# A graph convolution on one core: the search for runs moves from VectorE to ScalarE, and the sorted edges are searched in blocks of 8 instead of 16

## The reference, cut to what matters

```python
msg = node_feat[src] + edge_feat                       # 400000 x 64
agg = segment_sum(msg, dst, num_segments=12500)        # 12500 x 64
h = relu(agg @ W1 + b1)                                # 12500 x 128
x = layernorm(x + (h @ W2 + b2))
```

## Time and the profile before

| what | value |
|---|---|
| median of 3 runs | 1467.95 us (1467.6 to 1469.04) |
| profiled execution | 1467.16 us, its span 1465.4 us |
| TensorE matmul busy | 1223.0 us, 83% |
| VectorE busy | 1217.6 us, 83% |
| GpSimd busy | 967.6 us, 66% |
| ScalarE busy | 751.7 us, 51% |
| mean granted TensorE clock | 0.906 of full |

### The profile page before, as it was taken

How to read it: one execution, slowest core, us unless ns; L and a number is a source line. 1 busy time by engine, 2 the same in 40 slices (tenths; PEclk the granted TensorE clock), 3 DMA queues, 4 the chain that set the end, 5 groups by cost and what they waited for, 6 DMA issues and landing times.

```text
span 1465.4 us, 47112 instructions
## 1 busy us (share of the span) xinstructions
PE 1223.0 (83%) x18748; PEld 1107.5 (76%) x18749; DVE 1217.6 (83%) x2696; ACT 751.7 (51%) x941; POOL 967.6 (66%) x1043
## 2 busy tenths in 40 slices
PE   1457878888888899888989899999999999999873
PEld 1356777776778888887878889888888888898642
DVE  5499888898988898989998888888889899887333
ACT  3734322233445455554455666666666666665252
POOL 6767777777676677777767667676666766674132
PEclk8566698899998999999999999999999999999975
DMA  6724444444443444444443434444333444332132
GB/s 166 177 77 126 114 128 117 113 128 121 110 120 104 117 114 120 112 123 109 105 127 105 119 102 107 117 108 110 108 104 103 123 113 111 101 100 64 33 76 67
DMA packets 157980, 161.09 MB, mean 110 GB/s; under 512 B 52803, under 2 KB 141955, under 8 KB 157427
## 3 DMA queue, kind: packets, MB, share of 16 engines
q1 hardware_dynamic: 126149, 123.61, 28.6%
q0 software_dynamic: 31616, 34.50, 12.4%
HBM read 153.06 MB, written 4.93 MB: 108 GB/s over the span
## 4 chain that ended last, share of the span: by engine, by line
PE 44%; DVE 28%; issue 17%; DVEq 5%; ACT 3%; DMA 2%; POOL 1%; POOLq 0%; SPq 0%
PE sums_ps L1175 20%; PE counted_ps L1158 12%; DVE oh_key L953 11%; PE chunk_ps L1140 10%; DVE oh_lo L949 8%; DVEq L907 3%; ACT counts L741 3%; DVE lists L918 2%; DVE onehot L893 2%; DMA lists<-in_dst 1%; DVEq L918 1%; POOL x_parts L658 1%; DVE less_b L843 1%; DMA edge_records<-counts 1%; PE turn_ps L1186 1%
## 5 line engine op out<-in xcount | busy, mean ns | idle before, releaser
L617 POOL DMA_INDIRECT xmsg<-in_x,idx_t x925 | 888.4, 960 | 292.4 <-issue 275.0
L741 ACT CAST counts<-counted_ps 128x784 bf16<-128x784 f32 (+2 forms) x728 | 618.3, 865 | 500.8 <-PE counted_ps L1158 494.3
L1158 PE MATMUL counted_ps<-oh_key,oh_lo 128*128 128x98 bf16 (+1 forms) x5264 | 579.4, 232 | 143.6 <-DVE oh_key L953 109.5
L1175 PE MATMUL sums_ps<-x_parts,counts 128*128 128x193 bf16 (+3 forms) x4900 | 629.0, 254 | 0.3
L1158 PEld LDWEIGHTS counted_ps<-oh_key,oh_lo 128*128 128x128 bf16 x5264 | 381.8, 103 | 204.8 <-DVE oh_key L953 149.9
L949 DVE TENSOR_TENSOR oh_lo<-chunk_ps,tables 128x768 bf16<-128x768 f16 (+3 forms) x622 | 444.6, 715 | 94.6 <-PE counted_ps L1158 57.8
L953 DVE TENSOR_TENSOR oh_key<-chunk_ps,tables 128x1176 bf16<-128x1176 f16 (+2 forms) x622 | 459.5, 739 | 0.0
L1175 PEld LDWEIGHTS sums_ps<-x_parts,counts 128*128 128x128 bf16 (+3 forms) x4900 | 455.8, 118 | 4.6 <-issue 3.1
L1140 PE MATMUL chunk_ps<-onehot,cmsg 128*64 128x16 f32 (+4 forms) x4400 | 167.3, 222 | 6.3 <-DVE lists L918 5.3
L1140 PEld LDWEIGHTS chunk_ps<-onehot,cmsg 128*64 128x64 f32 x4400 | 153.6, 147 | 22.6 <-issue 9.5
L918 DVE TENSOR_TENSOR lists<-lists,chunk_ps 64x48 f32 (+6 forms) x625 | 113.8, 182 | 30.5 <-PE chunk_ps L1140 8.4
(11 more groups left out here) (104 smaller groups left out, 459.6 us busy)
## 6 DMA issues: line engine op xcount, KB each, us to landing
cmsg<-in_edge_attr SPq DMA_DIRECT2D x440, 160.0 KB
gmsg<-in_edge_attr SPq DMA_DIRECT2D x185, 160.0 KB
xmsg<-in_x,idx_t POOLq DMA_INDIRECT x925
x_parts<-in_x SPq DMA_DIRECT2D x12, 256.0 KB, 3.2
out_nodes<-x_parts SPq DMA_DIRECT2D x12, 256.0 KB, 2.6
edge_records<-counts SPq DMA_DIRECT2D x1, 1500.0 KB
lists<-in_src SPq DMA_DIRECT2D x1, 1400.0 KB
lists<-in_dst SPq DMA_DIRECT2D x1, 1400.0 KB
```

The costliest lines, as they stand in the source:

```text
L617: pool.indirect_dma_start(xmsg[:, at * D:(at + 1) * D], None, x, bass.IndirectOffsetOnAxis(ap=idx_t[:, of:of + 1], axis=0)).then_inc(gathe ...
L741: nc.scalar.copy(to.rearrange("p h (m n) -> p h m n", m=m), ps.rearrange("p m (n h) -> p h m n", h=HI)).then_inc(unit_kept, 1)
L1158: mm = nc.tensor.matmul(unit_ps[u][:, col:col + slot.key_cols], oh_lo[s % RING][:, n * P:(n + 1) * P], oh_key[s % RING][:, n * slot.key_co ...
L1175: mm = nc.tensor.matmul(sums_ps[0:n, 0:XC], counts[b % 2][:, h * P:h * P + n], x_parts[:, h * XC:(h + 1) * XC], start=(h == 0), stop=(h == ...
```

## The change

1. FINE goes from 16 to 8. A record row is half as long and there are twice as many; the array of largest destinations is twice as long (SPAN). A run of 128 edges is 16 rows instead of 8, and the same bytes. `plan` may put up to 121 edges into a window instead of 113, and makes another plan.
2. The count of the search moves from VectorE to ScalarE. ScalarE computes Sign(node - 0.5 - most) over the array and accumulates it: (blocks below) - (blocks not below). The values are written over the array in place, as bf16, so `less_b` is gone. As the sum is twice the count minus the length, the row number is used in half records (`record_halves`).
3. VectorE keeps the small instruction that makes the row number, now `locate`, at T-6. ScalarE's `search` stands at T-8, the load at T-15, and `load_records` at T-4.
4. For the first two groups ScalarE searches between its copies of `idx` and of `rel`, and VectorE locates after it has computed `rel`.
5. The five loads of weights and biases go from the start of SyncE's program to its end, after the last search, as `w1_sb`, `w2_sb` and `b2_all` now share memory with `most_b`.

```diff
-FINE = 16
+FINE = 8
...
-    SEARCH_LOAD = at_slots([(max(0, TABLE_AT[g] - 13), g) for g in later])
-    SEARCH = at_slots([(max(0, TABLE_AT[g] - 6), g) for g in later])
+    SEARCH_LOAD = at_slots([(max(0, TABLE_AT[g] - 15), g) for g in later])
+    SEARCH = at_slots([(max(0, TABLE_AT[g] - 8), g) for g in later])
+    LOCATE = at_slots([(max(0, TABLE_AT[g] - 6), g) for g in later])
...
+    record_halves = record_dram.rearrange("r (h k) -> (r h) k", h=2)
...
-        less_b = sb("less_b", [P, SPAN], bf16)
+        node_half = sb("node_half", [P, GROUPS])
...
+            sp.wait_ge(searched, GROUPS)
+            for half in range(2):
+                sp.dma_start(w1_sb[half * D:(half + 1) * D, :], w1).then_inc(weights_in, 16)
+            sp.dma_start(w2_sb[:, :], w2).then_inc(weights_in, 16)
+            sp.dma_start(b1_sb[:, :], b1.rearrange("(h o) -> h o", o=1)).then_inc(weights_in, 16)
+            sp.dma_start(b2_all[:, :], b2.rearrange("(o f) -> o f", o=1).broadcast_to([P, D])).then_inc(weights_in, 16)
             sp.wait_ge(block_summed, BLOCKS)
...
-                iota(run_list[:, r:r + n * t], [[0, n], [RUN, t]], 0, lists_made)
+                iota(run_list[:, r:r + n * t], [[0, n], [2 * RUN, t]], 0, lists_made)
...
-                for g in SEARCH.get(s - 3, []):
+                for g in LOCATE.get(s - 2, []):
                     load_records(g)
...
+            def search(g):
+                a, b = RANGES[g]
+                act.wait_ge(most_in[g % 2], 16 * (g // 2 + 1))
+                if g >= 2:
+                    act.wait_ge(run_ready, g - 1)
+                nc.scalar.activation(most_b[g % 2][:, 0:b - a].bitcast(bf16), most_b[g % 2][:, 0:b - a], ACT.Sign, bias=node_half[:, g:g + 1], scale=-1.0,
+                                     accum_out=found[g % 2][:, 0:1]).then_inc(searched, 1)
...
             for s in range(NS + 1):
+                for g in SEARCH.get(s, []):
+                    search(g)
                 for g in TURN_TABLE.get(s, []):
                     copy_tables(g)
...
-            def search(g):
+            def locate(g):
                 a, b = RANGES[g]
-                dve.wait_ge(most_in[g % 2], 16 * (g // 2 + 1))
-                nc.vector.tensor_scalar(less_b[:, 0:b - a], most_b[g % 2][:, 0:b - a], node_t[:, g:g + 1], 0.0, ALU.is_lt,
-                                        ALU.add, accum_out=found[g % 2][:, 0:1]).then_inc(searched, 1)
                 dve.wait_ge(searched, g + 1)
                 if g >= 2:
                     dve.wait_ge(records_in[g % 2], 16 * (g // 2))
-                nc.vector.scalar_tensor_tensor(out=run_at[g % 2][:, :], in0=found[g % 2][:, :], scalar=float(a),
+                nc.vector.scalar_tensor_tensor(out=run_at[g % 2][:, :], in0=found[g % 2][:, :], scalar=float(a + b),
                                                in1=run_t[:, g:g + 1], op0=ALU.add, op1=ALU.add).then_inc(run_ready, 1)
...
-                for g in SEARCH.get(s, []):
-                    search(g)
+                for g in LOCATE.get(s, []):
+                    locate(g)
                 for g in SUBTRACT.get(s, []):
                     subtract(g)
```

More of the change, by code:

```diff
@@ L202, in build @@
     assert UNITS[-1].first + UNITS[-1].nodes <= N and BLOCKS >= 4 and GROUPS <= P
-    SPAN = max(b - a for a, b in RANGES)
+    SPAN = -(-max(b - a for a, b in RANGES) // 2) * 2
     REC = 3 * FINE
@@ L206, in build @@
     PAD = max(0, max(RANGES[r // P][1] + RUN * j + RUN for r, (_, _, j) in enumerate(WINDOWS)) - CFINE)
-    assert PAD <= 5 * P
+    PAD_ROWS = -(-PAD // P)
+    PAD = PAD_ROWS * -(-PAD // PAD_ROWS)
+    assert PAD_ROWS <= 5
     DENSE = [u for u, x in enumerate(UNITS) if max(x.passes) * P > TOP]
@@ L324, in build @@
         chunk_out = sb("chunk_out", [ROWS, 2, TILES], i32)
-        w1_sb = sb("w1_sb", [P, HID])
-        w2_sb = sb("w2_sb", [HID, D])
+        w1_sb = most_b[0][:, 0:2 * HID].bitcast(f32)
+        w2_sb, b2_all = (most_b[1][:, 2 * k * D:2 * (k + 1) * D].bitcast(f32) for k in range(2))
+        assert SPAN >= max(2 * HID, 4 * D) and HID == P
         b1_sb = sb("b1_sb", [HID, 1])
-        b2_all = sb("b2_all", [P, D])
         eps = sb("eps", [P, 1])
@@ L517, in _ @@
             sp.dma_start(x_all[0:LAST, (HI - 1) * D:], x[(HI - 1) * P:, :]).then_inc(x_in, 16)
[L518 to L522, removed]
             sp.wait_ge(chunk_made, 2)
@@ L625, in load_records @@
                     pool.wait_ge(tables_turned, g - 1)
-                pool.indirect_dma_start(records[g % 2][:, :], None, record_dram,
+                pool.indirect_dma_start(records[g % 2][:, :], None, record_halves,
                                         bass.IndirectOffsetOnAxis(ap=run_at[g % 2][:, 0:1], axis=0)
@@ L703, in _ @@
                                ps[:, :, CROWS:ROWS]).then_inc(taken["idx"], 1)
+            def search(g):
[5 more added lines that the diff above has]
+                                     accum_out=found[g % 2][:, 0:1]).then_inc(searched, 1)
+            act.wait_ge(list_kept, 4)
+            for g in range(EARLY_GROUPS):
+                search(g)
             for g, (k, n, ps) in enumerate(turns("rel")):
@@ L837, in _ @@
             nc.vector.tensor_scalar(node_key[:, :], node_t[:, :], float(HI), -1.0, ALU.mult, ALU.add).then_inc(list_kept, 1)
-            dve.wait_ge(list_kept, 3)
-            def search(g):
+            nc.vector.tensor_scalar(node_half[:, :], node_t[:, :], 0.5, None, ALU.subtract).then_inc(list_kept, 1)
+            dve.wait_ge(list_kept, 4)
+            def locate(g):
                 a, b = RANGES[g]
-                dve.wait_ge(most_in[g % 2], 16 * (g // 2 + 1))
-                nc.vector.tensor_scalar(less_b[:, 0:b - a], most_b[g % 2][:, 0:b - a], node_t[:, g:g + 1], 0.0, ALU.is_lt,
-                                        ALU.add, accum_out=found[g % 2][:, 0:1]).then_inc(searched, 1)
                 dve.wait_ge(searched, g + 1)
@@ L859, in subtract @@
                                         float(8 * HI), ALU.subtract, ALU.min).then_inc(keys_ready, 1)
-            for g in range(EARLY_GROUPS):
-                search(g)
             link(nc.vector.tensor_reduce(least[:, :], dst_i.rearrange("t (s e) -> t s e", s=TILES), axis=AX.X, op=ALU.min))
@@ L1101, in _ @@
             turn("rel")
[L1102 removed]
+            pe.wait_ge(list_kept, 4)
             def turn_table(g, added_sums=0):
```

5 lines of the change are left out of this document (2 added, 3 removed).

## The result

The changed kernel takes 1452.55 us (median of 4 runs, 1451.0 to 1455.59), the kernel before 1468.13 us on the same chip. The ratio is 0.9896 with a 95% interval of 0.9877 to 0.9915: 15.6 us or 1.0% faster. The forecast was 1441 us in a range of 1418 to 1463. The direction and the range held; the gain was a little over half of the 27 us forecast.

A forecast was written before the change was run, and what follows sets the result against it. VectorE was taken to bound part A (nodes 0 to 2634), TensorE part B (the remaining slots). Part A -28 and part B +1 give -27: 1467.16 us becomes 1440, forecast 1441 us for the median, range 1418 to 1463.

The forecast's parts named there:

- VectorE's terms: VectorE's compares, searches and accumulator reads: fewer columns and no searches save 42 us in part A, 31 in part B.
- ScalarE's terms: ScalarE's 38 searches: 0.84 ns an entry plus fixed costs and reads, 58 us in all.
- TensorE's pass of width 3: TensorE's pass for the new width 3 slots in part B: 127 ns, between 85 ns and twice 85.
- What waits for the search, part B: ScalarE's copies queue behind 13 searches in part B, holding TensorE up 0.75 us each: +10 us.
- Part A: Slots covering nodes 0 to 2634, mostly width 1, bounded by VectorE: forecast to get 28 us shorter.
- -42 + 7 = -35 us of VectorE: VectorE in part A: 42 us of work saved, less 7 us of waits for ScalarE's searches.
- four fifths: Share of VectorE's 35 us saving in part A let through to the time: -28 us.
- The forecast of its own waits: GpSimd's waits for the row number in part A: down from 46 us to about 20.
- GpSimd takes over in A: Rival: GpSimd's gather pace limits part A's gain to 12 to 15 us, total 1455 us; chance 0.12.
- VectorE's wait at locate in A: VectorE waits at T-6 for ScalarE's search in part A: 0.3 us each, 24 times, +7 us.
- The rest at nothing: Record bytes, longer search loads, weight loads moved to SyncE's end, and the start: 0 us (start -2 to +2).

The follow-up runs named there:

- n2: Changed kernel with each chunk's gathers replaced by one plain load, and searches of groups 25 to 37 (part B) back on VectorE: 1437.58 us.
- n4: Changed kernel with each chunk's gathers replaced by one plain load, blocks of 8 kept, all searches back on VectorE: 1457.65 us, on another chip.
- n0: Kernel before the change, with each chunk's five gathers replaced by one plain load on SyncE's queue: 1461.11 us.
- n1: Changed kernel, with each chunk's five gathers replaced by one plain load on SyncE's queue: 1443.75 us.
- n3: Changed kernel with gathers replaced by plain loads, each ScalarE search moved to the last slot at or before T-8 with chunk jobs: 1419.28 us.
- f1: Changed kernel with blocks of 8 kept but all searches back on VectorE, gathers kept, slow chip: 2409.02 us, ratio 1.0057 to the kernel before.
- e1: Changed kernel with blocks of 8 kept but all searches back on VectorE, another slow chip: 2425.63 us, ratio 1.0004 to the kernel before.
- e2: Changed kernel with FINE back at 16, so only the search's move to ScalarE, slow chip: 2436.91 us, ratio 1.006 to the kernel before.
- e3: Changed kernel with the first search within the slots at slot 7 instead of 9, slow chip: 2411.85 us, ratio 0.9947 to the kernel before.
- g2: Changed kernel with the first in-slot search earlier and part B's searches back on VectorE, slow chip: 2393.34 us, ratio 1.0009 to the kernel before.

## Why the prediction was right, and by how much it was off

- *VectorE's terms*: as durations they were right, compares 37 us forecast and 36.9 measured, and no search is left. But the sum takes them as time of the engine, and the records of neighbouring instructions overlap. In the trace of the kernel before:

```profile
476.17 0.76 DVE L953 TENSOR_TENSOR oh_key<-chunk_ps,tables 128x1176 bf16<-128x1176 f16 x1
476.85 0.81 DVE L843 TENSOR_SCALAR_CACHE_REDUCE less_b<-most_b,node_t 128x584 bf16<-128x584 int16 x1
477.59 0.08 DVE L843 DVE_READ_ACCUMULATOR less_b<-most_b,node_t 128x1 f32 x1
```

The search starts 0.08 us before the compare's record ends, and the read of the accumulator, put down as 2.1 us in A and 1.2 in B, ends with the search's record. So VectorE's busy time fell by 622.7 - 585.6 = 37.1 us in A and by 525.5 - 496.3 = 29.2 in B, not by 42 and 31.
- *ScalarE's terms* were right: 58 us forecast, 52.4 + 7.4 = 59.8 measured, with int16 from SBUF at about the same rate: 1707 ns at 1691 entries and 1150 at 1017, 0.83 ns an entry.
- *TensorE's pass of width 3*, forecast at 127 ns: in these weight loads one pass with the three or four products behind it,

```profile
1240.53 0.10 PEld L1174 LDWEIGHTS counted_ps<-oh_key,oh_lo 128*128 128x128 bf16 x1
1240.62 0.34 PEld L1191 LDWEIGHTS sums_ps<-x_parts,counts 128*127 128x127 bf16 x3
1240.91 0.10 PEld L1174 LDWEIGHTS counted_ps<-oh_key,oh_lo 128*128 128x128 bf16 x1
```

(1240.91 - 1240.53) us less three products of 193 columns, taken at the 85 ns of a pass of 196, are 125 ns.
- *What waits for the search, part B*: +10 forecast for copies, +10.9 measured; -6 for VectorE's one-hots, -7.4 measured; in all +1 forecast and +2.6 measured. But not all 10.9 are the searches': with them on VectorE (n2, n4) TensorE still waits 22 to 23 us for copies where n0 has 17.8, and only 6 to 7 us go with them. The other 4 to 5 us came with the new plan and were put at nothing; that +10 and +10.9 agree is in part luck. The searches cost B 7 to 9 us in all, of which these waits are 6 to 7.
- *Part A*, -28 forecast, -21.1 measured. The term that was mis-sized is "-42 + 7 = -35 us of VectorE": its busy time fell by 37.1 us and its waits for the search were 9.6, so it gained 27.5. Of that 21.1 us came through, 77%, near the "four fifths" of the forecast. Without gathers VectorE gained 622.5 - 584.5 = 38.0, less 9.8 of waits, 28.2 us, and 26.7 came through, 95%; that this is near the -28 of the forecast is luck, as it is a larger share of a smaller saving. What GpSimd took, kept as a rival at 12 in 100 and not as a term, is 3.5 us by the waits and 5.6 by the two pairs of traces. The forecast of its own waits, about 20 us left, was right to 0.4 us, but 16.6 of them are one wait at the start.
- *The total* of 1452.55 us lies nearer to the 1455 of the rival "GpSimd takes over in A" than to the 1441 of the forecast, but not by that rival's sum: it has A gain 12 to 15 us, and A gained 21.1. The range held because it was wide enough for misses of one sign in all parts.
- *VectorE's wait at locate in A*, +7 forecast over 24 groups, 9.6 measured, 5.6 of them in the first group, where two 2.8 us copies stood ahead of the search. This place I had not looked at.
- *The rest at nothing*: the start cost 1.1 us and the tail 4.0. In the tail, the last block's 98 products take 10.01 us instead of 8.55, at a granted clock of 0.75 for 0.78; the rest I can't put down to a step. Without gathers the tails are 111.6 us in n0, and with the new plan 114.1 in n1 and n4, 113.7 in n3, but 111.1 in n2, at a clock of 0.80 for 0.77; so the plan itself isn't shown to lengthen it.

The gap of 13.6 us between -27 and the -13.4 of the span is thus 6.9 in A, 1.6 in B, 4.0 in the tail and 1.1 at the start. Two small misreadings have no weight: the earlier trace rows has 20.2 us of VectorE's waits for TensorE, not 20.3, and 63 slots have width 3, not 64.

## What to carry to other kernels

When work moves to an engine with room, its place in that engine's order is worth as much as the move: here the same search gave 15.6 us at a fixed distance from its use and 36.2 us when it was put where no copy is due and its result isn't needed yet. Take an engine's saving from its busy time in the stage and not from a sum of durations: here overlapping records and longer waits made 27.5 us of the 35 that were forecast. Before counting it in full, add up the engine with a fixed pace (here one gather in 1.25 us) over the stage, and ask where its waits lie: of 20.4 us in part A, 16.6 were one wait at the start. A change of two parts should be timed in halves: the new plan alone was worth 3.5 us. And where one execution differs from another by a few us in a stage, compare the granted clock and a second execution before naming a cause.

## What the runs showed of the hardware that was not expected

Four of the chips used ran the same kernel before in 2391 to 2423 us, two others in 1468 and 1469. On the slow ones TensorE crawls while GpSimd issues indirect DMAs. In f1 it does 12 and 6 matmuls in 5 us with four gathers, at a granted clock of 0.73 and 0.50, and 52 with none at 0.52, so the clock isn't what makes the difference. Over all slots of f1 TensorE starts 4.9 matmuls in a us while a gather runs and 10.1 otherwise; in the kernel before on a fast chip it is 13.9 and 14.5. The gathers' own time (0.94 us) and VectorE's and ScalarE's instructions were as on the others, the bytes moved too (166.8 MB in f1 and in the changed kernel), and with the gathers gone such a chip ran n0 in 1461.11 us. Why TensorE slows down there isn't settled. A ratio that was taken on one kind of chip says little about the other: the edits of e1, e2, e3 and g2 moved the time by 0.6% at most where the gathers are the bound.
